# Attention A's score products in two halves of 64 queries, and attention B's maxima placed set by set

## The reference

```python
# attention A: 32 heads of 128, 8 key/value heads, 4-bit codes times scales
q = hidden_states @ _dequant(q_codes, q_scales)       # k, v the same way, then rope on q and k
causal = jnp.tril(jnp.ones((s, s), dtype=bool))
mask = jnp.where(causal, 0.0, -jnp.inf).astype(q.dtype)
scores = jnp.einsum('bhqd,bhkd->bhqk', q, k) * scale + mask[None, None]
attn = jax.nn.softmax(scores, axis=-1)
out = jnp.einsum('bhqk,bhkd->bhqd', attn, v)
return out.transpose(0, 2, 1, 3).reshape(b, s, NH * HD) @ _dequant(o_codes, o_scales)
# experts: 8 of rank 64, the best two of each token
gate_probs = jax.nn.softmax(x @ gate_w.T, axis=-1)
weights, sel = jax.lax.top_k(gate_probs, TOP_K)
for e in range(N_EXPERTS):
    out = out + w_full[:, e:e + 1] * (x @ lora_A[e].T @ lora_B[e].T)
# attention B: 32 heads of 16, 8 key/value heads, causal, same form as A
```

## Time and profile before

| | us |
|---|---|
| median of 3 runs | 951.85 (951.2 to 951.88) |
| the profiled execution | 950.79 |
| span of its profile | 949.1 |
| PE busy | 912.1 |
| DVE, POOL, ACT busy | 771.8, 618.9, 598.8 |

### The profile page before, as it was taken

One profiled execution on the slowest core, in us unless ns is written; L12 is line 12 of the kernel. 1 busy time (PEld: TensorE's weight loads), 2 busy tenths in 40 slices (PEclk: granted clock), 3 DMA queues, 4 the chain that ended last, 5 costly groups with the idle time before them and its releaser, 6 DMA issues.

```text
span 949.1 us, 19791 instructions
## 1 busy us (share of the span) xinstructions
PE 912.1 (96%) x6698; PEld 487.6 (51%) x6698; DVE 771.8 (81%) x1812; ACT 598.8 (63%) x1323; POOL 618.9 (65%) x668
## 2 busy tenths in 40 slices
PE   5889999999999999999999999999999989999998
PEld 3445555555555555545555555554445534444543
DVE  6888887887887788788788878898878879996764
ACT  4677666676667567666576756646463469997331
POOL 4788876968777687687777777822368744553211
PEclk9999999999999999999999999999999999999999
DMA  9177376484665556647557465464332943121145
GB/s 339 51 182 173 87 185 145 63 211 107 122 186 88 144 116 157 144 86 199 117 101 190 83 144 144 87 175 84 76 82 55 163 80 64 42 43 24 23 86 159
DMA packets 256005, 114.10 MB, mean 120 GB/s; under 512 B 244144, under 2 KB 244784, under 8 KB 251312
## 3 DMA queue, kind: packets, MB, share of 16 engines
q1 hardware_dynamic: 246416, 70.42, 39.1%
q10 hardware_dynamic: 9504, 42.49, 12.9%
HBM read 49.84 MB, written 2.10 MB: 55 GB/s over the span
## 4 chain that ended last, share of the span: by engine, by line
PE 76%; DVE 10%; ACT 6%; issue 3%; DMA 3%; POOL 1%; SPq 1%; ACTq 0%; DVEq 0%; POOLq 0%
PE bank L1253 16%; PE bank L1255 16%; PE bank L1254 16%; PE bank L1734 4%; PE bank L1352 3%; PE bank L1354 3%; PE bank L1353 3%; PE bank L1372 3%; PE bank L1374 3%; PE bank L1373 3%; ACT bank L989 2%; PE bank L1666 2%; DVE bw_hi L1981 2%; DVE bank L1964 2%; PE bank L1640 2%
## 5 line engine op out<-in xcount | busy, mean ns | idle before, releaser
L622 POOL TENSOR_TENSOR rt<-rt 128x512 f32<-128x512 f32 x80 | 101.6, 1273 | 131.8 <-DVE rt L1949 131.8
L1981 DVE SCALAR_TENSOR_TENSOR bw_hi<-bank,rden,bw_hi 128x128 f16<-128x128 f32 (+3 forms) x256 | 123.3, 544 | 60.9 <-ACT bw_hi L1025 60.9
L989 ACT ACTIVATE bank<-bank,shift,c_score 128x128 f32<-128x128 f32 (+3 forms) x256 | 147.3, 605 | 2.1
L1964 DVE CUSTOM_DVE_ANT_0 bank<-bank,mask_w 128x512 f32<-128x512 f32 (+3 forms) x256 | 117.9, 520 | 21.5 <-PE bank L1354 21.5
L1025 ACT ACTIVATE bw_hi<-bank,rden 128x128 f16<-128x128 f32 (+3 forms) x256 | 114.5, 535 | 22.4 <-DVE rden L1974 22.2
L984 ACT ACTIVATE shift<-smax,c_score 128x4 f32<-128x4 f32 x64 | 19.0, 297 | 155.4 <-DVE smax L1964 155.4
L629 POOL TENSOR_TENSOR arena<-rt,arena 128x512 f16<-128x512 f32 x80 | 92.4, 1158 | 8.6 <-ACT arena L973 7.8
L1253 PE MATMUL bank<-xt,wq_hi 128*128 128x512 f16 x256 | 97.0, 379 | 0.0
L1254 PE MATMUL bank<-xt,wq_hi 128*128 128x512 f16 x256 | 97.0, 379 | 0.0
L1255 PE MATMUL bank<-xt,wq_lo 128*128 128x512 f16 x256 | 97.0, 379 | 0.0
L1253 PE MATMUL bank<-wo_hi,arena 128*128 128x512 f16 x256 | 97.0, 379 | 0.0
(11 more groups left out here) (241 smaller groups left out, 2453.6 us busy)
## 6 DMA issues: line engine op xcount, KB each, us to landing
qcode<-in_q_codes ACTq DMA_DIRECT2D x7, 1024.0 KB, 5.0
qscale<-in_q_scales ACTq DMA_DIRECT2D x7, 1024.0 KB, 7.2
ocode<-in_o_codes ACTq DMA_DIRECT2D x7, 1024.0 KB, 4.9
oscale<-in_o_scales ACTq DMA_DIRECT2D x7, 1024.0 KB, 7.9
kvcode<-in_k_codes ACTq DMA_DIRECT2D x8, 256.0 KB, 7.5
kvcode<-in_v_codes ACTq DMA_DIRECT2D x8, 256.0 KB, 7.9
kvscale<-in_k_scales ACTq DMA_DIRECT2D x8, 256.0 KB, 8.1
kvscale<-in_v_scales ACTq DMA_DIRECT2D x8, 256.0 KB, 8.9
```

Of the source, the lines that this page charges most:

```text
L989: act.activation(a_rows(i, s), a_rows(i, s), ACT.Exp, bias=shift[:, s % 2, c:c + 1], scale=c_score[:, 0:1], accum_out=bank[3][:, SUMS_AT + ...
L1964: dve.tensor_tensor_reduce(bank[bk][:, o:o + (i + 1) * P], bank[bk][:, o:o + (i + 1) * P], mask_w[:, S - (i + 1) * P:S], 1.0, LOWEST, ALU. ...
L1981: dve.scalar_tensor_tensor(out=p_row[:, s % 2, LO_AT[i]:LO_AT[i] + P_STEP * i + 1:P_STEP], in0=turned_back(i, s), scalar=rden[:, s % 2, c: ...
```

## The change

**Score products.** `scores` makes each term as two products with 64 stationary columns. Half f = 0 has the tile's first 64 queries against 128 i + 64 keys, half f = 1 the others against 128 (i + 1). Each half writes 64 of the 128 output partitions. In tiles 0 and 1 (`SWAPPED`) the first half goes to partitions 64 to 127 and the second to 0 to 63; to fit, the tokens of these tiles are exchanged by halves on the host, exchanged back in the transposes ahead of attention A's and the experts' use (`in_order`), given a mask of their own (`back_w`), and written to the output in two DMAs for each tile. Both halves count in the semaphore `s_ps`. At the first s of all, eight products of 128 columns fill the places that no half writes.

```diff
+SWAPPED = (0, 1)
...
+        def in_order(a, t):
+
+            return a.rearrange("p (f n) -> p f n", f=2)[:, ::-1] if t % ST in SWAPPED else a
...
-                    pe.matmul(o_ap, q_hi[:, s, qs], k_hi[:, b, 0:w], start=True, stop=False)
-                    pe.matmul(o_ap, q_hi[:, s, qs], k_lo[:, b, 0:w], start=False, stop=False)
-                    mm = pe.matmul(o_ap, q_lo[:, s, qs], k_hi[:, b, 0:w], start=False, stop=True)
-                    if i != 0:
-                        mm.then_inc(s_ps, 1)
+                    if first and s == 0 and i in SWAPPED:
+                        for c0 in range(0, S, P):
+                            pe.matmul(bank[bk][:, c0:c0 + P], mask_w[:, 0:P], mask_w[:, 0:P], start=True, stop=True)
+
+                    halves = [(i * P + f * P // 2, (1 - f if i in SWAPPED else f) * P // 2, i * P + (f + 1) * P // 2)
+                              for f in range(2)]
+                    terms = ((q_hi, k_hi), (q_hi, k_lo), (q_lo, k_hi))
+                    for k, (qa, ka) in enumerate(terms):
+                        for q0, r0, keys in halves:
+                            mm = pe.matmul(bank[bk][r0:r0 + P // 2, o:o + keys], qa[:, s, q0:q0 + P // 2],
+                                           ka[:, b, 0:keys], start=(k == 0), stop=(k == len(terms) - 1))
+                            if i != 0 and k == len(terms) - 1:
+                                mm.then_inc(s_ps, 1)
...
-                sp.dma_start(o_out[:, t, :], x[:, t, :]).then_inc(d_out, 16)
+                for f in range(2):
+                    r = (1 - f if t % ST in SWAPPED else f) * P // 2
+                    sp.dma_start(o_out[f * P // 2:(f + 1) * P // 2, t, :], x[r:r + P // 2, t, :]).then_inc(d_out, 16)
```

```diff
             turn_max(0, 0)
-            place_max(0, 0)
+            place_max(sp, 0, 0)
             turn_max(0, 1)
-            place_max(0, 1)
+            turn_queries(NT - 2)
             turn_max(1, 0)
-            turn_queries(NT - 2)
-            place_max(1, 0)
+            place_max(sp, 1, 0)
             turn_max(1, 1)
             turn_queries(NT - 1)
-            place_max(1, 1)
-            turn_max(2, 0)
...
+            for q in range(2, SETS):
                 turn_max(q, 0)
                 turn_max(q, 1)
-                place_max(q, 0)
-                place_max(q, 1)
-                if q < 5:
+                place_set(q)
+                if 3 <= q < 5:
                     turn_keys(NT - 5 + q)
```

```diff
                 gate_weights(ph, 0)
-                if ph == 0:
-                    w_factors(1)
                 rows_low(ph, 0)
                 rows_low(ph, 1)
                 gate_choice(ph, 1)
+                if ph == 0:
+                    w_factors(1)
                 gate_weights(ph, 1)
                 rows_low(ph, 2)
```

More of the change, by code:

```diff
@@ L430, in build @@
         d_mrows = [[sem(f"d_mrows{c}{i}") for i in range(2)] for c in range(2)]
+        d_mset = [sem(f"d_mset{i}") for i in range(2)]
+        d_mfirst = [[sem(f"d_mfirst{c}{i}") for i in range(2)] for c in range(2)]
         d_q, d_k = ([sem(f"{n}{i}") for i in range(2)] for n in ("d_q", "d_k"))
@@ L459, in m_place, with max_turned, place_max @@
             return n % 3, 16 * (n // 3 + 1)
+        def max_turned(q, c):
+            return (d_mfirst[c][q], 16) if q < 2 else (d_mturn[c], 16 * (q - 1))
+        def place_max(eng, q, c):
+            j, b = set_place(q)
+            eng.wait_ge(*max_turned(q, c))
+            for f in range(2):
+                two = slice(f * P // 2 + MAX_AT, f * P // 2 + MAX_AT + 2)
+                eng.dma_start(qt_b[two, 2 * j + c, b * S:(b + 1) * S], m_turned[two, q % 2, c]
+                              ).then_inc(d_mrows[c][q], 16)
+        def in_order(a, t):
+            return a.rearrange("p (f n) -> p f n", f=2)[:, ::-1] if t % ST in SWAPPED else a
         def rows_landed(c, t):
@@ L586, in _ @@
             pool.memset(mask_w[:, 0:S - P], 0.0).then_inc(consts, 1)
+            pool.memset(back_w[:, 0:P], 0.0).then_inc(consts, 1)
             pool.wait_ge(consts, 4)
@@ L1230, in _ @@
             for q in range(SETS + 2):
-                if q < SETS:
+                if q == 0:
+                    b_exps(q, range(2))
+                    place_max(act, q, 1)
+                    b_exps(q, range(2, LOADS - 2))
+                elif q < SETS:
                     b_exps(q, range(LOADS - 2))
@@ L1261, in ln_t @@
                 for k in range(KT):
-                    mm = pe.transpose(bank[LN_BANK[c][t]][:, k * P:(k + 1) * P],
+                    mm = pe.transpose(in_order(bank[LN_BANK[c][t]][:, k * P:(k + 1) * P], t),
                                       xn[:, t % 2, k * P:(k + 1) * P], ident[:])
@@ L1543, in turn @@
                 for k in range(KT):
-                    mm = pe.transpose(bk[:, k * P:(k + 1) * P], src[:, k * P:(k + 1) * P], ident[:])
+                    mm = pe.transpose(in_order(bk[:, k * P:(k + 1) * P], m), src[:, k * P:(k + 1) * P], ident[:])
                 mm.then_inc(mt_ps, 1)
@@ L1653, in b_keys @@
                     pe.wait_ge(bexp, load - 1)
-                if step in (0, 2):
-                    pe.wait_ge(d_mrows[step // 2][q % 2], 32 * (q // 2 + 1))
+                if q < 2 and step in (0, 2):
+                    pe.wait_ge(d_mrows[step // 2][q], 32)
+                elif step == 0:
+                    pe.wait_ge(d_mset[q % 2], 32 * (q // 2))
                 if load == 0:
@@ L2122, in _ @@
             dve.tensor_copy(mask_b, mask_f[:])
+            dve.tensor_copy(back_w[:, P:2 * P], back_f[:])
             rope(0, ("q", 0))
@@ L2442, in even_odd, with by_halves @@
         return w.reshape(-1, heads, A_HD // 2, 2).swapaxes(2, 3).reshape(w.shape)
+    def by_halves(v):
+        v = v.reshape(B, ST, 2, P // 2, D).copy()
+        for t in SWAPPED:
+            v[:, t] = v[:, t, ::-1]
+        return v.reshape(B, S, D)
     def by_group(w):
```

45 lines of the change are left out of this document (24 added, 21 removed).

## The result

| | us | ratio to before | 95% interval |
|---|---|---|---|
| before, same chip | 951.87 (951.2 to 953.12) | | |
| after, 4 runs | 958.87 (955.51 to 960.12) | 1.0074 | 1.0051 to 1.0097 |
| before, another chip session | 950.51 (949.29 to 954.0) | | |
| after again, 6 runs | 956.66 (954.87 to 958.04) | 1.0056 | 1.0038 to 1.0074 |

The changed kernel is slower, by 0.74% and 0.56%; the two intervals overlap. The forecast was 955.1, in a range of 945.5 to 961.5. Its profiled execution took 955.51 with a span of 953.7, 4.6 us above the span of before.

A forecast was written before the change was run, and what follows sets the result against it. PE was taken to bound the kernel, busy 96% of the span. Terms 5.6 - 1.6 - 1.2 + 0.5 = +3.3 on the profiled 950.79 gave 954.1, the median 1.1 above: 955.1 us, range 945.5 to 961.5.

The forecast's parts named there:

- Price of the two changes of form: Attention A: switching between 64- and 128-column products costs 0.22 us for one s, +14.1 us over 64.
- Saving of the sides: Attention A: column sides run independently and share the shortened work equally, saving 0.14 us for one s, -9.0 us over 64.
- Attention A in all: Attention A: price of form changes, saving, extra changes and products, less time beside waits, together +5.6 us.
- The part that lies beside PE's waits: Attention A: some of the added cost falls where PE would have stood anyway, -1.0 us.
- Experts: Experts: `rows_low` moves up, so PE's 1.98 us wait at the first `lora_b` product shrinks, -1.6 us.
- the wait less what tile 2 keeps of it: Experts: the first `lora_b` wait goes, except a part that reappears at the third tile, -1.6 us.
- Attention B: Attention B's start: one of three waits for placed rows goes, less half a microsecond from the moved turn, -1.2 us.
- the third rival: Attention B: `place_set` comes too late, PE waits at step 0 in fourteen sets, +4.2 us; 959.4 us, chance 0.12.
- End: Kernel end: two DMAs store each token tile, only the last extra issue on the path, +0.5 us.
- the free change: Attention A: rival that changing the array's form costs nothing, sum -10.9, 940.9 us; chance 0.14.
- the strict order: Attention A: rival that products keep program order, so no saving, sum +12.3, 964.2 us; chance 0.06.
- All waits vanish: Experts and attention B: rival that waits and slow stretches vanish whole, -3.8 and -6.2, giving 948.0 us; chance 0.14.

The follow-up runs named there:

- noswap: The kernel after with no tile's halves exchanged (`SWAPPED` empty), half 0 always in the lower 64 partitions: 964.46 us, ratio 1.0146.
- tile3: Before, with only tile 3's score products in halves, without exchange, maxima and stores as before: 964.19 us in one execution.
- bp_wmid: b_pair plus `w_factors(1)` placed between `rows_low` of tile 0 and of tile 1: 947.6 us against 950.89 of before, ratio 0.9964.
- stores2: Before, with each token tile's output stored by two DMAs of 64 partitions: 954.38 us in one execution.
- blocks: a_only, but each tile's three half 0 products written first, then the three of half 1: 954.48 us in one execution.
- a_only: Before plus only the score products in halves with exchange, masks and two stores for a token tile: 954.12 us, ratio 1.0037.
- w_only: Before with only `w_factors(1)` moved behind `gate_choice` of the last four tiles: 951.56 us, ratio 0.9996.
- b_pair: Before plus attention B's new start (two placements on ACT's queue, turn of queries moved), later sets placed by pair: 948.77 us, ratio 0.9981.
- b_act: b_pair with `turn_queries` of tile 6 back behind `turn_max(1, 0)`, where before has it: 949.67 us, ratio 0.999.

## Why the prediction was right

The range held, 958.87 and 956.66 in 945.5 to 961.5, and so did the direction. The size didn't: +3.2 us was forecast for the median, and +7.0 and +6.1 were measured. Step by step:

- **Price of the two changes of form**: 0.22 taken, 0.226 measured (in noswap 0.093 at the entry, 0.010 in the first product after, 0.123 between the two first starts, which holds the exit; in tile3 0.093 and 0.133). Right, and right for its reason: the nearest rows were a true analogue, and the transpose with 3 columns was not. The 0.015 for weight loads at the entry stood on no row, and the entry has nothing beyond its 0.095; the way back cost 0.133 where 0.11 was taken, so two small errors offset each other.
- **Saving of the sides**: 0.14 taken, 0.152 measured (noswap less after). Right, and the exchange is what makes it. The pair of them, +0.074 for an s, is 4.7 us over 64.
- **Attention A in all**: +5.6 taken, +4.4 measured up to 655 us (+0.8 and +3.6). The part that lies beside PE's waits was taken at 1.0; from 60 to 660 us PE stood 6.4 us before (600 less 593.57 busy) and 5.2 after (594.84), by the windows with the columns of the earlier trace rows. Before:

```profile
60.00:660.00 600.00, 593.57 (x3834) 328.02 (x3832) 495.24 (x1238) 393.99 (x979) 436.44 (x367) 1.00 0.58 133
```

After:

```profile
60.00:660.00 600.00, 594.84 (x4547) 336.69 (x4546) 490.80 (x1228) 391.82 (x977) 435.11 (x365) 1.00 0.58 132
```

- **Experts**: -1.6 taken, -0.3 measured, and that with before's slow stretch gone: +1.4 to the kernels of the same clock. The step that failed: "the wait less what tile 2 keeps of it". -1.6 leaves tile 2 some 0.4 of the 1.98 us. It kept all: by the starts, PE loses 2.14 us at the first tile in before, and 0.36 there and 1.80 at the third tile in after. And three waits for DVE follow that before doesn't have, by the starts 0.27 and 0.57 us for `x` and 0.46 more for `xn`, together the 1.3. I had left out who else reads `w_factors`: ACT's scaling of the later weights waits for `inv_w`, and the high part of the fourth tile is queued behind it. That this is what makes DVE late is argued; with `w_factors(1)` ahead of tile 1's rows instead (bp_wmid) the waits for `x` are gone and 0.48 for `xn` is left. Waits of PE in after from 660 to 752 us (total, times, longest):

```profile
PE bank L1280 <- DMA mt<-m_stack: 1.8, 2, 1.6
PE bank L1289 <- DVE xn L1896: 0.5, 1, 0.5
PE bank L1280 <- DVE x L2257: 0.4, 1, 0.4
```

- **Attention B**: -1.2 taken, -0.3 (and -0.9) measured, as the difference of two terms that I had both named and priced wrongly together. The start gave 2.9, but 1.7 of it is before's slow stretch at 776; the waits alone gave 1.2. Placement by set took 2.6 and 2.0: the third rival's mechanism was at work in every trace with `place_set`, at a lower price than its 4.2 us, since only late turns use up the 0.4 us of margin. Giving it a chance of 0.12 as an event was the error; a term of some 2 us in the sum would have been right. The "about 1.2 us" of ACT's issuing for a placement was 2.0 and 1.6.
- **End**: +0.5 taken, +0.8 measured (after, after again, stores2).
- **Profile and median**: the sum was made against a profile with three slow stretches and gives 954.1 for one; after's profile, with none, took 955.5, and the medians 958.87 and 956.66. What I left out is that stretches come and go between executions of one kernel; in 28 runs before lay between 948.7 and 954.8. And that the profile came out so near the sum is luck: its +4.6 holds 3.4 us of slow clock that before had where PE works and it hadn't. With the clock alike the sections add up to +8.0 against the +3.3 of the sum: experts 3.0, attention B 2.6 and the end 0.3 worse than taken, attention A 1.2 better. The medians, +7.0 and +6.1, bear that out.

Of the rivals, the free change and the strict order are out by tile3 and by blocks. "All waits vanish" happened in part: no slow stretch, and the placement waits at the start down by 2 us, but not in the sum.

The start of attention B deserves a word of caution: a_only and blocks have the old start and show -3.0 there too, w_only -1.4, stores2 -0.5, before 0. The old start is one of luck; the new one gave 2.8 to 3.2 in all seven kernels that have it whole. Nor has any of the seven a slow stretch there, while three of the six kernels with the old start have one (before, w_only, stores2). What the new start brings on average is what b_pair measures, 1.7 to 2.0 us, shorter waits and less slow clock together.

## What to carry to other kernels

A product on half of the array's columns costs nothing by its count, but each change between halves and whole costs about a tenth of a microsecond, so halves pay only where many stand together; make both sides equally long, and it doesn't matter in which order they are written. Joining two waits into the earlier one spends the later one's slack: with the turns landing at 2.3 us and now and then at over 4, keep the waits apart or count a late landing for every few sets. Before moving a small operation off one reader's path, list all its readers on every engine.

## What the runs showed of the hardware

- Products on different column halves start as soon as their own side is free, whatever the order in which they are written (1.601 and 1.608 us for an s).
- Most turns of maxima land 2.3 us after their issue, but nine of the 32 in before and seven of the 32 in after take 2.9 to 4.5.
- The half-clock stretches are not bound to a place. At the first `lora_b` product one began within 1.3 us of a PE wait of 2.0 us in five of nine traces, and of a wait of 0.2 us in none of five; others stood at 14, 34, 72 and 772 to 779 us. What else decides it is open.
- One placement of two DMAs takes 1.6 to 2.0 us of ACT's queue (in after 1.44 and 0.58 us, then 0.57 and 1.06), and more by the wait for the turn: ACT stood idle for 3.16 us in b_act.
